# Cross attention 0 of a four-layer decoder: the negated maxima are added on four 32-row tiles, for both halves at once and ahead of the scores

## The chip, the cores and the metric

One NeuronCore of one Trainium2 chip runs the whole program. The metric is the time on the device of one execution, in microseconds (us). The engines of the core work side by side and wait for each other by semaphores: TensorE (PE in the profile, PEld for its weight loads), VectorE (DVE), ScalarE (ACT), GpSimd (POOL) and SyncE (SP), which only issues transfers here.

## The reference, cut to what matters

A decoder of four layers, each with self attention, cross attention and a feed-forward part. The change lies in the cross attention of layer 0: 1024 queries against 6404 keys, 16 heads of 64 numbers.

```python
def _L0_xattn_ref(q_in, k_in, v_in, key_mask, Wq, bq, Wk, bk, Wv, bv, Wo, bo):
    HEADS, QSIZE, KSIZE = (16, 64, 64)
    ...
    qw = (q_in @ Wq + bq).reshape(B, M, HEADS, QSIZE)
    kw = (k_in @ Wk + bk).reshape(B, N, HEADS, QSIZE)
    vw = (v_in @ Wv + bv).reshape(B, N, HEADS, KSIZE)
    a = jnp.einsum('bmhd,bnhd->bhmn', qw, kw) / jnp.sqrt(jnp.float32(QSIZE))
    a = jnp.where(key_mask[:, None, None, :], a, -jnp.inf)
    a = jax.nn.softmax(a, axis=-1)
    o = jnp.einsum('bhmn,bnhd->bmhd', a, vw).reshape(B, M, HEADS * KSIZE)
    return o @ Wo + bo
```

Before each exponential the row's maximum is subtracted. In the kernel the scores stand transposed (keys on partitions, queries along the free axis), so the maximum of a query can't be the bias of an activation. It is added to the scores on TensorE instead.

## The kernel before

The function is `cross_0`. The 16 heads are worked as `P = 8` pairs; the two heads of a pair, `a = 0` and `1`, lie on partitions 0 to 63 and 64 to 127 (`head(a)`). The keys come in `C = 13` chunks of up to 512 (four tiles of 128 keys, the last chunk of a pair has three; 51 tiles for a pair, 408 in all, numbered `t`). The queries come in two halves of 512 (`HALVES`).

The order of the work is written out by hand. `turns()` goes over turns `g`. In turn `g` the chunk `g` of a first pass is done, which finds the maxima from bfloat16 copies of the keys and queries (`maxima`, L2235, eight groups of 128 queries for each chunk, reduced by VectorE in L2417), and beside it chunk `j = g - 14` of the second pass. So turns 0 to 13 hold maxima alone, turns 14 to 103 both, and turns 104 to 117 the second pass alone. A turn has one step `s` for each tile of chunk `j`, usually with two of the eight groups of maxima. For each tile TensorE does:

- `scores(j, s, half)` for both halves: two float32 products of 64 rows (L2248), which run at the same time since they lie on different rows of the array, into banks `2 * half` and `2 * half + 1` of PSUM; then two bfloat16 products of 64 rows (L2250) that add the negated maxima: the stationary operand is `ones`, the moving one `Qa`, which holds the negated maximum of each query as a sum of two bfloat16 numbers in rows 0 and 1 of each head and zeros in the other rows.
- `products(t - 1)` (L2267): the exponentials of the tile before times the values, four float32 products with 64 columns of the array, two at a time.

ScalarE takes the exponential of each half (L2354) into `Pr`, which has four buffers. GpSimd adds it to the running sums `Ps0` (L2474) and `Ps1` (L2483). A group of maxima in turns 14 on uses banks 4 and 5 alone, so that the next one, or the new keys and values (L2274, L2279, in step 0 of each turn), must wait for its reduction. At the end of a turn VectorE merges its maxima (L2449); at the end of a pair's 13 turns it negates them (L2453) and splits them into `mz` (L2457, L2459), and TensorE turns them into rows (L2293), from which `Qa` is copied.

In step 0, and in a step with other work of the pair (queries, rows, sums, output), the second group of maxima stands between the two halves of the scores; in the others it stands behind them. "The usual step" below is one of turns 14 to 103 with no such work.

Of the kernel before, what the change touches and what calls it, by code (L numbers as in the profile page):

```python
# [12 lines left out]
ALU = mybir.AluOpType  # L13
# [12 lines left out]
HALVES = [slice(h * HALF, (h + 1) * HALF) for h in range(S // HALF)]  # L26
# [2137 lines left out]
def cross_0(k, io, X, stack):  # L2164
# [6 lines left out]
    nc, ps, ctx = k.nc, k.ps, k.context  # L2171
# [13 lines left out]
    Kr, Kb = k.tile(stack, "Kr", [128, 16, CHUNK]), k.tile(stack, "Kb", [128, 2, CHUNK], BF16)  # L2185
    Vc = k.tile(stack, "Vc", [128, 3, CHUNK])
    Q, Qb = k.tile(stack, "Q", [128, 3, S]), k.tile(stack, "Qb", [128, 2, S], BF16)
    Qa, ones = k.tile(stack, "Qa", [128, 2, S], BF16), k.tile(stack, "ones", [128, 128], BF16)
# [3 lines left out]
    mx, red, neg = k.tile(stack, "mx", [128, 8, 2]), k.tile(stack, "red", [128, 2, 8, 2]), k.tile(stack, "neg", [128, 8, 2])  # L2192
    mz = k.tile(stack, "mz", [128, 8, 2, 64], BF16)
    ones_f, zero_row = k.tile(stack, "ones_f", [128, 64]), k.tile(stack, "zero_row", [1, HALF], BF16)
    out_bias = k.tile(stack, "out_bias", [128, 1])
    head = lambda a: slice(64 * a, 64 * a + 64)
# [4 lines left out]
    def turns():  # L2201

        for g in range(-1, N + LAG + 3):
            j = g - LAG
            yield g, j, (ctx.tiles_in(j % C) if 0 <= j < N else TPC)

    def maxima_at(g, s, steps):
        return range(8 * s // steps, 8 * (s + 1) // steps) if 0 <= g < N else range(0)

    def maxima_bank(i, q):  # L2210
        return (4, 0, 2)[(8 * i + q) % 3] if i < LAG else 4

    def pair_for(g, s, turn, step):

        p = (g - turn) // C
        return p if s == step and (g - turn) % C == 0 and 0 <= p < P else None

    def pe():
        taken = {0: [], 2: [], 4: []}

        def take_banks(b, *when_free):

            for mark in taken[b]:
                nc.tensor.wait_ge(*mark)
            taken[b] = when_free
# [12 lines left out]
        def scores(j, s, half):  # L2238
            t, p = KT * (j // C) + TPC * (j % C) + s, j // C
            if s == 0 and half == 0:  # L2240
                nc.tensor.wait_ge(*key_set.at(j + 1))
                if j % C == 0:
                    nc.tensor.wait_ge(*query_set.at(p + 1))
                    nc.tensor.wait_ge(*rows_set.at(p + 1))
            take_banks(2 * half, exp_done.at(2 * t + half + 1))
            sl = HALVES[half]
            for a in range(2):
                nc.tensor.matmul(ps[:, 2 * half + a, :], lhsT=Kr[head(a), j % 16, s * 128:(s + 1) * 128], rhs=Q[head(a), p % 3, sl], start=True, stop=False)  # L2248
            for a in range(2):
                mm = nc.tensor.matmul(ps[:, 2 * half + a, :], lhsT=ones[head(a), :], rhs=Qa[head(a), p % 2, sl], start=False, stop=True)  # L2250
            mm.then_inc(*scored.up())

        def products(t):
# [59 lines left out]
        for t in range(P):  # L2313
            mm = nc.tensor.matmul(ps[:, 0, 0:1], lhsT=wo[:, t, :], rhs=bv[:, t:t + 1], start=t == 0, stop=t == P - 1)
# [4 lines left out]
        for g, j, steps in turns():  # L2319
            for s in range(steps):  # L2320
                t = KT * (j // C) + TPC * (j % C) + s
                items = maxima_at(g, s, steps)
                others = [(item, pair_for(g, s, turn, step)) for item, turn, step in
                          ((queries, -1, 1), (rows, C, 1), (sums, LAG + C, 1), (output, LAG + C + 2, 2)) if pair_for(g, s, turn, step) is not None]
                between = 2 if s == 0 or others else 1
                for q in items[:1]:
                    maxima(g, q)
                if 0 <= j < N:
                    scores(j, s, 0)
                for q in items[1:between]:  # L2330
                    maxima(g, q)
                if 0 <= j < N:
                    scores(j, s, 1)
                for q in items[max(1, between):]:
                    maxima(g, q)
                if s == 0:
                    keys_and_values(g + 1, j + 1)
                for item, p in others:
                    item(p)
                if 0 <= j and 0 < t <= KT * P and (j < N or s == 0):  # L2340
                    products(t - 1)
# [55 lines left out]
    def dve():  # L2397
        nc.vector.memset(ones[:], 1.0)
        nc.vector.memset(ones_f[:], 1.0)
        nc.vector.memset(zero_row[:], 0.0).then_inc(*zeroed.up())  # L2400
        nc.vector.memset(mz[:], 0.0).then_inc(*zeroed.up())
        nc.vector.wait_ge(*constant_mm.at(1))
        nc.vector.tensor_tensor(out_bias[:], ps[:, 0, 0:1], bo[:], ALU.add).then_inc(*constant_set.up())
        both = ps[:, 4:6, :]

        def inverse(p, n):
            sl = slice(n * 128, (n + 1) * 128)
            nc.vector.wait_ge(*sums_set.at(p + 1))
            nc.vector.reciprocal(over[:, sl], over[:, sl]).then_inc(*inverse_step.up())

        for g, j, steps in turns():
            for s in range(steps):
                for q in maxima_at(g, s, steps):
                    nc.vector.wait_ge(*maxima_mm.at(8 * g + q + 1))
                    if g >= 2 and q == 0:
                        nc.vector.wait_ge(*merged.at(g - 1))
                    nc.vector.tensor_reduce(red[:, g % 2, q, :], ps[:, maxima_bank(g, q):maxima_bank(g, q) + 2, 0:ctx.keys_in(g % C)], AX, ALU.max).then_inc(*reduced.up())  # L2417
                p = pair_for(g, s, -1, 1)
                if p is not None:
                    nc.vector.wait_ge(*query_mm.at(p + 1))  # L2420
                    if p >= 3:
                        nc.vector.wait_ge(*scored.at(2 * KT * (p - 2)))
                        nc.vector.wait_ge(*query_copied.at(p - 2))
                    nc.vector.tensor_scalar(Q[:, p % 3, :], both.rearrange("p a n -> p (a n)"), bq[:, p:p + 1], scale, ALU.add, ALU.mult).then_inc(*query_set.up())
                for n in range(8):
                    p = pair_for(g, s, LAG + C + (n + 2) // 4, (n + 2) % 4)
                    if p is not None:
                        inverse(p, n)
                p = pair_for(g, s, LAG + C + 2, 1)
                if p is not None:  # L2430
                    nc.vector.wait_ge(*inverse_step.at(9 * p + 8))
                    nc.vector.wait_ge(*acc_copied.at(p + 1))
                    nc.vector.tensor_tensor(Ur[:], Ur[:], over[:], ALU.mult).then_inc(*inverse_step.up())
                p = pair_for(g, s, LAG + C + 2, 2)
                if p is not None:
                    nc.vector.wait_ge(*out_mm.at(p + 1))
                    if p:
                        nc.vector.wait_ge(*x_added.at(p))
                        nc.vector.tensor_tensor(X[:], X[:], both.rearrange("p a n -> p (a n)"), ALU.add).then_inc(*x_added.up())
                    else:  # L2440
                        nc.vector.wait_ge(*constant_set.at(1))
                        nc.vector.scalar_tensor_tensor(X[:], both.rearrange("p a n -> p (a n)"), out_bias[:, 0:1], X[:], ALU.add, ALU.add).then_inc(*x_added.up())
            if 0 <= g < N:
                nc.vector.wait_ge(*reduced.at(8 * (g + 1)))
                if g % C == 0:
                    nc.vector.tensor_copy(mx[:], red[:, g % 2]).then_inc(*merged.up())
                else:
                    nc.vector.wait_ge(*merged.at(g))
                    nc.vector.tensor_tensor(mx[:], mx[:], red[:, g % 2], ALU.max).then_inc(*merged.up())  # L2449
                if g % C == C - 1:  # L2450
                    p = g // C
                    nc.vector.wait_ge(*merged.at(g + 1))
                    nc.vector.tensor_scalar(neg[:], mx[:], -1.0, None, ALU.mult).then_inc(*rows_step.up())  # L2453
                    nc.vector.wait_ge(*rows_step.at(3 * p + 1))
                    if p:
                        nc.vector.wait_ge(*rows_mm.at(p))
                    nc.vector.tensor_copy(mz[:, :, :, 0], neg[:]).then_inc(*rows_step.up())  # L2457
                    nc.vector.wait_ge(*rows_step.at(3 * p + 2))
                    nc.vector.tensor_tensor(mz[:, :, :, 1], neg[:], mz[:, :, :, 0], ALU.subtract).then_inc(*rows_step.up())  # L2459

    def pool():
        for g, j, steps in turns():
# [811 lines left out]
```

## Time and the profile before

| | |
|---|---|
| median of 3 runs | 6965.2 us (6961.23 to 6971.22) |
| the profiled execution, its own time | 6964.83 us |
| its span, first to last instruction | 6963.1 us |
| mean granted TensorE clock | 0.904 of full |
| TensorE busy in the span | 5944.1 us, 85% |
| the second pass of cross attention 0 | from about 697 to 2945 us |

A row of the timeline gives the start (us from the span's start), the time from there to the end of the last instruction merged into it, the engine, line and operation, and the count. Matmuls overlap: one of 512 columns lasts about 0.38 us in the records, but the next starts about 0.21 us after it. So what a matmul costs is read from start to start, not from its own duration. A float32 matmul has two records.

### The profile page before, as it was taken

The numbers are of one execution on the slowest core, as the hardware profiler recorded it, in microseconds if no ns is written. First come the engines' busy times: TensorE is split into PE (matmuls) and PEld (weight loads), VectorE is DVE, ScalarE is ACT, GpSimd is POOL, SyncE is SP. The second block draws the span as 40 slices with busy tenths as digits, with TensorE's granted clock in tenths as the row PEclk, the third lists the DMA queues.
The fourth block names the chain that finished last, engine by engine and source line by source line (L and its number), as shares of the span: only waits on it lengthen the run. The fifth ranks groups of instructions, "written<-read, shape, count | busy, mean of one in ns | idle before, by whom it ended". The sixth has DMA issues, their size and how long they took to land. (4 is left out here: it accounts for less than half of the span.)

```text
span 6963.1 us, 76588 instructions
## 1 busy us (share of the span) xinstructions
PE 5944.1 (85%) x30204; PEld 2276.6 (33%) x30219; DVE 3275.8 (47%) x4563; ACT 3212.5 (46%) x3531; POOL 1903.2 (27%) x845
## 2 busy tenths in 40 slices
PE   8975999999999999979869569998888368888879
PEld 5741333333333333336624121111356111111114
DVE  4557555555555553034363430000232799899813
ACT  3321444444444445422202249998111137777752
POOL 0000878788787889900000000000000000000000
PEclk8875999999999999989989789999776679999979
DMA  1000000000000000000021030000000300000000
GB/s 47 4 13 0 1 1 1 1 1 1 1 1 1 1 1 1 1 28 7 9 92 34 17 101 16 16 9 7 16 30 8 118 1 9 18 9 9 2 17 31
DMA packets 91699, 118.19 MB, mean 17 GB/s; under 512 B 23358, under 2 KB 66729, under 8 KB 89741
## 3 DMA queue, kind: packets, MB, share of 16 engines
q1 hardware_dynamic: 91340, 113.29, 5.2%
q8 instruction: 240, 3.93, 0.2%
q14 instruction: 119, 0.97, 0.0%
HBM read 75.86 MB, written 37.39 MB: 16 GB/s over the span
## 5 line engine op out<-in xcount | busy, mean ns | idle before, releaser
L2417 DVE TENSOR_REDUCE red<-ps 128x2 f32<-128x1024 f32 (+1 forms) x832 | 976.9, 1182 | 965.7 <-PE ps L2235 963.8
L2354 ACT ACTIVATE Pr<-ps,key_bias 128x1024 f32<-128x1024 f32 x816 | 897.5, 1115 | 1112.9 <-PE ps L2250 1112.5
L2474 POOL TENSOR_TENSOR Ps<-Ps,Pr 128x1024 f32<-128x1024 f32 x400 | 944.1, 2360 | 318.0 <-ACT Pr L2354 318.0
L2910 DVE TENSOR_REDUCE red<-ps 128x2 f32<-128x1024 f32 (+2 forms) x1102 | 961.4, 926 | 79.3 <-PE ps L2825 66.2
L2483 POOL TENSOR_TENSOR Ps<-Ps,Pr 128x1024 f32<-128x1024 f32 x400 | 948.4, 2371 | 32.7 <-ACT Pr L2354 32.7
L492 POOL MEMSET sel<- 16x2048 f32 (+1 forms) x2 | 2.7, 1368 | 3402.9 <-POOLq L89 3402.9
L2888 ACT ACTIVATE Pr<-ps 128x1024 f32<-128x1024 f32 x816 | 786.2, 1021 | 224.6 <-PE ps L2835 223.6
L2248 PE MATMUL ps<-Q,Kr 64*128 64x512 f32 x3264 | 851.8, 600 | 0.0
L2267 PE MATMUL ps<-Pr,Vc 128*64 128x512 f32 x3264 | 789.8, 605 | 0.0
L3011 ACT ACTIVATE Pr<-ps 128x1536 f32<-128x1536 f32 x544 | 732.7, 1495 | 2.7 <-PE ps L2977 2.3
L2825 PE MATMUL ps<-Kp,Q 52*128 52x512 bf16 (+1 forms) x1664 | 449.8, 410 | 226.8 <-DVE red L2910 149.3
L2235 PE MATMUL ps<-Kb,Qb 64*128 64x512 bf16 (+1 forms) x1664 | 335.7, 406 | 149.3 <-DVE red L2417 115.4
L2848 PE MATMUL ps<-Pr,V 128*9 128x512 f32 x3264 | 435.0, 605 | 0.0
L2990 PE MATMUL ps<-Pr,V 128*8 128x512 f32 x3264 | 427.1, 596 | 0.2 <-ACT Pr L3011 0.2
L2977 PE MATMUL ps<-Q,Kp 48*128 48x512 bf16 x1632 | 329.3, 385 | 56.9 <-ACT Pr L3011 33.3
L2835 PE MATMUL ps<-Q,Kp 52*128 52x512 bf16 x1632 | 363.5, 386 | 12.2 <-ACT Pr L2888 11.6
L2825 PEld LDWEIGHTS ps<-Kp,Q 52*128 52x128 bf16 x1664 | 107.1, 94 | 799.8 <-DVE red L2910 713.2
L2248 PEld LDWEIGHTS ps<-Q,Kr 64*128 64x128 f32 x3264 | 311.8, 191 | 161.5 <-issue 122.7
L3020 DVE COPY Oc<-ps 128x512 f32<-128x512 f32 x8 | 5.5, 692 | 732.7 <-PE ps L2990 732.7
L2267 PEld LDWEIGHTS ps<-Pr,Vc 128*64 128x64 f32 x3264 | 198.0, 136 | 382.0 <-issue 290.8
L2250 PE MATMUL ps<-Qa,ones 64*128 64x512 bf16 x1632 | 313.3, 380 | 0.0
L2235 PEld LDWEIGHTS ps<-Kb,Qb 64*128 64x128 bf16 x1664 | 80.5, 95 | 665.2 <-DVE red L2417 421.0
(487 smaller groups left out, 6596.9 us busy)
## 6 DMA issues: line engine op xcount, KB each, us to landing
L_dram_K<-parts SPq DMA_DIRECT2D x26, 384.0 KB, 2.8
Kp<-L_dram_K SPq DMA_DIRECT2D x16, 624.0 KB
L_dram_K<-parts SPq DMA_DIRECT2D x26, 256.0 KB, 2.3
Kp<-L_dram_K SPq DMA_DIRECT2D x16, 416.0 KB
w<-L_ffn_experts_w_dram SPq DMA_DIRECT2D x24, 256.0 KB, 3.0
L_dram_V<-Vt SPq DMA_DIRECT2D x13, 258.0 KB, 2.8
Vc<-L_dram_V SPq DMA_DIRECT2D x13, 258.0 KB, 2.7
ctx<-ctx_dram SPq DMA_DIRECT2D x13, 256.0 KB, 5.8
```

The lines of the kernel that those rows point to most:

```text
L2248: nc.tensor.matmul(ps[:, 2 * half + a, :], lhsT=Kr[head(a), j % 16, s * 128:(s + 1) * 128], rhs=Q[head(a), p % 3, sl], start=True, stop=False)
L2267: mm = nc.tensor.matmul(ps[head(a), 6 + half, :], lhsT=Vc[:, j % 3, at:at + 64], rhs=Pr[:, t % 4, half, a, :], start=False, stop=True, ski ...
L2354: nc.scalar.activation(Pr[:, t % 4, half].rearrange("p a n -> p (a n)"), ps[:, 2 * half:2 * half + 2, :].rearrange("p a n -> p (a n)"), AC ...
L2417: nc.vector.tensor_reduce(red[:, g % 2, q, :], ps[:, maxima_bank(g, q):maxima_bank(g, q) + 2, 0:ctx.keys_in(g % C)], AX, ALU.max).then_inc ...
L2474: nc.gpsimd.tensor_tensor(into, into, src, ALU.add).then_inc(*summed0.up())
L2483: nc.gpsimd.tensor_tensor(into, into, src, ALU.add).then_inc(*summed1.up())
L2825: mm = nc.tensor.matmul(ps[:, b + item - first, 0:keys], lhsT=Q[head(a), p, q * 128:(q + 1) * 128], rhs=Kp[head(a), p % 3, at:at + keys], ...
L2848: mm = nc.tensor.matmul(ps[at:at + 9, 6, :], lhsT=A.V[:, kt, 2 * p + a, :], rhs=Pr[:, t % 4, half, a, :], start=False, stop=True, skip_gro ...
L2888: nc.scalar.activation(Pr[:, t % 4, half].rearrange("p a n -> p (a n)"), ps[:, 2 * half:2 * half + 2, :].rearrange("p a n -> p (a n)"), AC ...
L2910: nc.vector.tensor_reduce(red_flat[:, g % 2, first:first + n], ps[:, b:b + n, 0:ctx.keys_in(g % C)], AX, ALU.max).then_inc(*reduced.up())
L2990: mm = nc.tensor.matmul(ps[at:at + 8, 6 + p % 2, :], lhsT=A.V[:, kt, 2 * p + a, :], rhs=Pr[:, i % 18, :], start=False, stop=True, skip_gro ...
L3011: nc.scalar.activation(Pr[:, slot:slot + n, :].rearrange("p a n -> p (a n)"), ps[:, 3 * (u % 2):3 * (u % 2) + n, :].rearrange("p a n -> p ...
```

## The change

All four additions of the negated maxima of a tile (two heads, two halves) are done ahead of the scores, each on a 32-row tile of the array: rows 0 to 31 and 64 to 95 for the first half, 32 to 63 and 96 to 127 for the second. For that the two rows of `mz` are written twice, at 0 and 1 and at 32 and 33. The additions now begin the sum in each bank and the scores end it. The banks of both halves are waited for ahead of the additions.

```diff
-            take_banks(2 * half, exp_done.at(2 * t + half + 1))
-            sl = HALVES[half]
+            if half == 0:
+                take_banks(0, exp_done.at(2 * t + 1))
+                take_banks(2, exp_done.at(2 * t + 2))
+                for quarter in range(4):
+                    x, a = quarter // 2, quarter % 2
+                    rows = slice(64 * a + 32 * x, 64 * a + 32 * x + 32)
+                    nc.tensor.matmul(ps[:, quarter, :], lhsT=ones[rows, :], rhs=Qa[rows, p % 2, HALVES[x]], start=True, stop=False)
             for a in range(2):
-                nc.tensor.matmul(ps[:, 2 * half + a, :], lhsT=Kr[head(a), j % 16, s * 128:(s + 1) * 128], rhs=Q[head(a), p % 3, sl], start=True, stop=False)
-            for a in range(2):
-                mm = nc.tensor.matmul(ps[:, 2 * half + a, :], lhsT=ones[head(a), :], rhs=Qa[head(a), p % 2, sl], start=False, stop=True)
+                mm = nc.tensor.matmul(ps[:, 2 * half + a, :], lhsT=Kr[head(a), j % 16, s * 128:(s + 1) * 128], rhs=Q[head(a), p % 3, HALVES[half]], start=False, stop=True)
             mm.then_inc(*scored.up())
...
-                    nc.vector.tensor_copy(mz[:, :, :, 0], neg[:]).then_inc(*rows_step.up())
+                    twice = neg[:].unsqueeze(3).to_broadcast([128, 8, 2, 2])
+                    parts = mz[:].rearrange("p q a (x r) -> p r q a x", r=32)
+                    nc.vector.tensor_copy(parts[:, 0], twice).then_inc(*rows_step.up())
                     nc.vector.wait_ge(*rows_step.at(3 * p + 2))
-                    nc.vector.tensor_tensor(mz[:, :, :, 1], neg[:], mz[:, :, :, 0], ALU.subtract).then_inc(*rows_step.up())
+                    nc.vector.tensor_tensor(parts[:, 1], twice, parts[:, 0], ALU.subtract).then_inc(*rows_step.up())
```

On TensorE, the order of a step 0 and of the usual step behind it, before the change (L2235 are maxima, L2248 scores, L2250 the additions, L2274 and L2279 new keys and values, L2267 the products):

```order
574 L2235 MATMUL ps<-Kb,Qb 128x512 x2
575 L2248 MATMUL ps<-Q,Kr 128x512 x2
576 L2250 MATMUL ps<-Qa,ones 128x512 x2
577 L2235 MATMUL ps<-Kb,Qb 128x512 x2
578 L2248 MATMUL ps<-Q,Kr 128x512 x2
579 L2250 MATMUL ps<-Qa,ones 128x512 x2
580 L2274 MATMUL ps<-ctx_masked,Wk 128x512
581 L2279 MATMUL ps<-Wv,ctx 128x128 x4
582 L2267 MATMUL ps<-Pr,Vc 64x512 x4
583 L2235 MATMUL ps<-Kb,Qb 128x512 x2
584 L2248 MATMUL ps<-Q,Kr 128x512 x2
585 L2250 MATMUL ps<-Qa,ones 128x512 x2
```

The same two steps on TensorE after the change (L2251 are the additions, L2253 the scores, L2277 and L2282 keys and values, L2270 the products):

```order
553 L2235 MATMUL ps<-Kb,Qb 128x512 x2
554 L2251 MATMUL ps<-Qa,ones 128x512 x4
555 L2253 MATMUL ps<-Q,Kr 128x512 x2
556 L2235 MATMUL ps<-Kb,Qb 128x512 x2
557 L2253 MATMUL ps<-Q,Kr 128x512 x2
558 L2277 MATMUL ps<-ctx_masked,Wk 128x512
559 L2282 MATMUL ps<-Wv,ctx 128x128 x4
560 L2270 MATMUL ps<-Pr,Vc 64x512 x4
561 L2235 MATMUL ps<-Kb,Qb 128x512 x2
562 L2251 MATMUL ps<-Qa,ones 128x512 x4
563 L2253 MATMUL ps<-Q,Kr 128x512 x4
```

The two pairs of additions have become one group of four, between the first maxima and the first scores. In the usual step both halves of the scores now follow each other (L2253 x4), and the group of four stands where the scores of the first half began.

## Rows read from the trace of the kernel before

**Rows 1.** The page: busy time of each engine, and the group of the additions.

```profile
PE 5944.1 (85%) x30204; PEld 2276.6 (33%) x30219; DVE 3275.8 (47%) x4563; ACT 3212.5 (46%) x3531; POOL 1903.2 (27%) x845
...
L2250 PE MATMUL ps<-Qa,ones 64*128 64x512 bf16 x1632 | 313.3, 380 | 0.0
```

**Rows 2.** Stretch and its length, busy PE, PEld, DVE, ACT, POOL, granted clock, DMA.

```profile
965.00:2700.00 1735.00, 1617.35 (x8320) 589.41 (x8318) 905.31 (x781) 823.75 (x860) 1411.02 (x616) 0.99 0.00 1
2750.00:2900.00 150.00, 150.00 (x734) 54.47 (x732) 1.22 (x1) 76.61 (x75) 150.00 (x66) 1.00 0.00 1
```

**Rows 3.** Timeline of a usual step and the start of the next.

```profile
1703.65 0.39 PE L2235 MATMUL ps<-Kb,Qb 64*128 64x512 bf16 x2
...
1703.88 1.02 PE L2248 MATMUL ps<-Q,Kr 64*128 64x512 f32 x4
...
1704.73 0.38 PE L2250 MATMUL ps<-Qa,ones 64*128 64x512 bf16 x2
...
1704.95 1.02 PE L2248 MATMUL ps<-Q,Kr 64*128 64x512 f32 x4
1705.16 2.19 ACT L2354 ACTIVATE Pr<-ps,key_bias 128x1024 f32<-128x1024 f32 x2 [2.42 <-PE ps L2250]
...
1705.81 0.38 PE L2250 MATMUL ps<-Qa,ones 64*128 64x512 bf16 x2
...
1706.03 0.38 PE L2235 MATMUL ps<-Kb,Qb 64*128 64x512 bf16 x2
...
1706.33 1.94 PE L2267 MATMUL ps<-Pr,Vc 128*64 128x512 f32 x8
...
1708.20 0.39 PE L2235 MATMUL ps<-Kb,Qb 64*128 64x512 bf16 x2
```

**Rows 4.** Timeline, TensorE: the step with the one-row products that clear a pair's sums.

```profile
706.21 0.40 PE L2235 MATMUL ps<-Kb,Qb 64*128 64x512 bf16 x2
706.54 0.60 PE L2260 MATMUL ps<-zero_row 1*128 1x512 bf16 x2
707.07 1.94 PE L2267 MATMUL ps<-Pr,Vc 128*64 128x512 f32 x8
```

**Rows 5.** Timeline, TensorE: a step of the second pass alone.

```profile
2933.44 1.13 PE L2248 MATMUL ps<-Q,Kr 64*128 64x512 f32 x4
2934.40 0.38 PE L2250 MATMUL ps<-Qa,ones 64*128 64x512 bf16 x2
...
2937.66 0.70 PE L2248 MATMUL ps<-Q,Kr 64*128 64x512 f32 x2
```

**Rows 6.** Timeline of a step 0, with VectorE and GpSimd around it.

```profile
1694.54 2.36 POOL L2474 TENSOR_TENSOR Ps<-Ps,Pr 128x1024 f32<-128x1024 f32 x1
...
1695.77 1.16 DVE L2449 TENSOR_TENSOR mx<-mx,red 128x16 f32<-128x16 f32 x1
...
1696.27 0.39 PE L2235 MATMUL ps<-Kb,Qb 64*128 64x512 bf16 x2
...
1696.85 1.21 DVE L2417 TENSOR_REDUCE red<-ps 128x2 f32<-128x1024 f32 x1
...
1698.12 0.39 PE L2235 MATMUL ps<-Kb,Qb 64*128 64x512 bf16 x2 [0.39 <-DVE red L2417]
...
1699.83 1.12 PE L2274 MATMUL ps<-ctx_masked,Wk 128*128 128x512 f32 x2 [0.25 <-DVE red L2417]
...
1706.35 2.36 POOL L2474 TENSOR_TENSOR Ps<-Ps,Pr 128x1024 f32<-128x1024 f32 x1 [2.52 <-ACT Pr L2354]
...
1708.66 2.35 POOL L2483 TENSOR_TENSOR Ps<-Ps,Pr 128x1024 f32<-128x1024 f32 x1
```

**Rows 7.** Timeline: the last sums of the second pass.

```profile
2951.81 3.68 PE L2302 MATMUL ps<-Ps,ones_f 128*64 128x512 f32 x8 [8.15 <-POOL Ps L2483]
```

**Rows 8.** Timeline: the end of a pair's maxima.

```profile
952.86 2.29 DVE L2457 CAST mz<-neg 128x16 bf16<-128x16 f32 x1
...
956.57 0.61 PE L2235 MATMUL ps<-Kb,Qb 64*128 64x512 bf16 x2 [5.50 <-DVE red L2417]
```

## The prediction

> **What bounds the kernel now.** I read the page first, then busy time by stretch, then the timeline of single steps. The page gives the size of what is changed: 1632 additions of the negated maxima, in pairs, so 816 starts on TensorE [rows 1]. In 965 to 2700 us, where both passes run, TensorE is busy 1617 of 1735 us, GpSimd 1411, VectorE 905 and ScalarE 824; in 2750 to 2900 us, where the second pass runs alone, both TensorE and GpSimd are busy all 150 us [rows 2]. These are two limits, and the change is worth something else in each.
>
> In the usual step TensorE waits for nobody. From start to start [rows 3]: first maxima to scores 0.23 us, scores of a half 0.85 or 0.86 (four passes, two at a time, 0.43 each), additions 0.22, scores 0.86, additions 0.22, and 2.38 from the first maxima to the second. Then 0.30 to the products and 1.87 for them; 4.55 in all. The exponentials of the tile end at 1707.35 (1705.16 + 2.19) and the next step starts at 1708.20, so ScalarE has 0.85 us in hand there.
>
> In step 0 it is another engine. The second maxima stand 1.85 us behind the first (1696.27, 1698.12) and new keys 1.71 behind those (1699.83), both with an idle time that a reduction ended, since only one pair of banks is left for maxima [rows 6].
>
> **What a change of tile shape costs.** Additions cost 0.22 from start to start where they stand among scores of the same shape [rows 3]. Maxima (64 rows by 128 columns) to products (128 by 64) takes 0.30, not 0.22. The nearest row to what the change brings is another: maxima to a one-row product, whose tile is 32 rows high, 706.21 to 706.54, 0.33 us (the second of the two maxima is 0.02 late there, so 0.31), and from the second of the one-row pair (which run one after the other, 0.60 for the two less 0.38 for one, so it starts 0.22 later) at 706.76 to the products 0.31 [rows 4]. So going over to a 32-row tile costs about 0.09 more than an ordinary step, as does leaving it. A float32 product that comes first after such a change also shows its weight load: in the second pass alone the first half's scores take 0.96 (2933.44 to 2934.40) against 0.85 [rows 3, 5]; 0.10 more. The first bfloat16 pair behind a change takes 0.01 more (0.23 against 0.22) [rows 3].
>
> The row shows a change from 64 to 32 rows that costs as much as one to column tiles. The Trainium skill, "TensorEngine Tiling (Array Packing)", Key Properties, says that changing the tiling mode, not just the tile, drains TensorE: by that rule the change pays two drains for each tile, and the trace agrees with 0.09 us for one. The page "TensorE: Matmul & The Clock Gate" of the Trainium skill, Measured speedup vs the span model, gives 3.07 times for four row tiles of 32 rows, not 4; an estimate by it would be 4 x 0.22 / 3.07 = 0.28 us for the group of four, 0.06 more than I take, 14 us over 240 steps.
>
> **The change part by part.**
>
> *The additions.* Removed: one start of 0.22 in each tile, since four run at once and not two by two. The trace has no four row tiles at once. Lower bound of the group: 0.22, as for a pair whose two members start within 0.01 of each other; upper bound: two pairs one after the other 0.44, or four singles 0.86, as the one-row pair runs when both use the same rows [rows 4]. These four use four different quarters of the rows and four banks, so I take 0.22 and keep 0.44 for the range.
>
> *The changes of shape.* Added: 0.09 into the 32-row tiles and 0.09 out, 0.10 for the weight load of the float32 scores that is now bare, 0.01 for the first bfloat16 group: 0.29. By the second decimals above, first maxima to second maxima goes from 2.38 to 0.32 + 0.32 + 0.96 + 0.86 = 2.46 or 2.47. Net **+0.09 us for a usual step**; the removal is worth less than the two changes of shape it brings.
>
> *How many such steps.* Turns 14 to 103 are 90 chunks, six pairs of 51 tiles and 12 chunks of four, 354 tiles. 90 are step 0; 24 have other work (queries, rows, sums, output, six each). That leaves 240, and the trace has 240 steps of the pattern of rows 3. 240 x 0.09 = **+22 us**.
>
> *Step 0 and steps with other work.* The path on TensorE from first to second maxima goes from 1.30 to 0.32 + 0.32 + 0.96 = 1.60 or 1.61. It is still below 1.85, so the reduction hides it; if the group of four took 0.44 it would be 1.83, just hidden too. From second maxima to new keys TensorE has 0.22 less work, which lengthens the wait for the reduction and gives nothing. **0 us.** The steps of the chunks with 260 keys have short reductions: about +0.1 in each of some seven, below 1 us.
>
> *GpSimd behind it.* Once per chunk GpSimd runs dry and starts again with the first exponential of step 1 (idle 2.52 before 1706.35); from there each sum takes 2.31 (1706.35 to 1708.66) [rows 6]. The merge of the maxima at the end of the turn lasts 1.16 us, until GpSimd's running sum ends at 1696.90 (1694.54 + 2.36), and the reduction of step 0 starts with that end, at 1696.85, 0.58 behind its maxima. From the second maxima to the new keys, with nothing else in the way of the reduction, it is 1.71 in all; from the first to the second it is 1.85, so the merge makes it 0.14 late. This is the path that sets step 0. After the change the first scores are ready 0.31 later behind the first maxima (1.61 against 1.30), so GpSimd starts 0.31 later in each chunk; and a step of 4.64 is now longer than two sums, 4.62, so it waits 0.02 to 0.04 more in each of two steps. Its sum then ends 0.31 to 0.38 later in a chunk, where the three TensorE steps alone give 0.09 x 2.67 = 0.24. I add 0.07 in 90 chunks: **+6 us**, between 0 and 12.
>
> *The second pass alone.* 54 tiles. There the step leaves one shape and enters another anyway and the bare load is there already: -0.22 + 0.09 + 0.01 + small = -0.11 for TensorE, 54 x 0.11 = -6 us. But its last sums waited 8.15 us for GpSimd [rows 7], which is busy throughout [rows 2] at 4.62 a tile against TensorE's 4.22 (2933.44 to 2937.66) [rows 5]. TensorE will wait 14 us and not 8. **0 us**; if GpSimd were not there, -6.
>
> *The wait for both halves.* The additions wait for both exponentials of the tile before; behind them on TensorE stand all scores of the tile, and ScalarE waits for those. In the usual step they are done 0.85 + 0.32 = 1.17 us ahead of the additions, and in the second pass alone 0.64 ahead (they start 0.43 behind the additions [rows 3], so 2934.40 + 0.43 + 2.19 = 2937.02 against 2937.66 [rows 5]). No time; were the cover gone, it would be up to one exponential, 1.1, in each tile.
>
> *VectorE.* `mz` is written with 32 numbers and not 16, eight times. The cast took 2.29 us at the end of a pair for 16 numbers, since it waits until a sum of GpSimd ends, and TensorE then waited 5.50 for the reduction behind it [rows 8]. Some 16 more numbers are hundredths of a us. If the repeated source took the cast out of that wait, it would give back up to 2.1 x 6 = 13 us; I see no reason that it should. **0 us**, between -13 and 0.
>
> *The sum*: 22 + 0 + 6 + 0 = +28 us. The profiled execution took 6964.83 us, 0.4 below the median of 6965.2, so 6964.8 + 28 = **6993 us**, 0.4% slower. Less than 0.2% (14 us) can't be told from no change here.
>
> **The rivals.**
>
> - *The four don't run at once* (two and two, or each start later). For it: nothing in the trace shows four. Against: pairs on separate rows start within 0.01. At 0.44 the usual step has +0.31: 240 x 0.31 = 74, plus 6, 7045 us; one after another beyond 7150. Chance 0.10 for the first and 0.02 for the second; another 0.1 for a part of it, 0.03 to 0.08 a group, 7000 to 7015.
> - *Faster: rows can be re-tiled without a stop* (only column tiles would cost it). Then both 0.09 and the bare load fall away and the usual step has 0.22 less: 240 x -0.22 = -53, 6912 us. It decides from the point where two changes and the load cost less than 0.22. Against it stand the 0.31 into and out of the one-row product [rows 4]. Chance 0.04; 0.02 more for the mix of it with a cheaper cast.
> - *No change: the load is not bare* (the float32 weights go in beside the additions, which use other quarters at their turn), or one of the two stops is hidden. Then the usual step has -0.01 to 0.00, and what is left is GpSimd's later start and noise: 6964 to 6975 us. For it: the way out of 32-row tiles into float32 scores is nowhere in the trace. Against: each first float32 product behind a change shows it [rows 5]. Chance 0.11.
> - *The change as forecast*: 0.61.
>
> **How the numbers follow.** The time is that of the likeliest case, whose own range is 6984 to 7002. The range of 8 in 10 leaves out the faster case, most of the "no change" case (together below 6974: 0.10) and the two-and-two case above 7025 (0.10): 6974 to 7025. Slower by over 0.2% (above 6979): forecast and the rival of the four, 0.83; same 0.11; faster 0.06.
>
> **What the profile will show.** In the usual step: four additions that start within about 0.02 of each other; maxima to additions and additions to scores 0.32 each; the first pass of the scores 0.53 and the second 0.43; a step of 4.64. In step 0 the same 1.85 to 1.9 and 1.71. The last sums wait some 14 us for GpSimd. The cast of `mz` near 2.3. The prediction is wrong if the additions start one after the other, or if they stand 0.22 from their neighbours.

## The result, and the profile after

| | before | after |
|---|---|---|
| median | 6965.2 us (6958.39 to 6971.49, 7 runs) | 6992.56 us (6986.86 to 7017.58, 7 runs) |
| profiled execution: span | 6963.1 us | 6990.9 us |
| first maxima of cross attention 0 start | 530.5 us | 521.6 us |
| second pass: first scores to last sums | 696.7 to 2954.4, 2257.7 us | 688.3 to 2983.6, 2295.3 us |

The ratio is 1.0048, 95% interval 1.0033 to 1.0064: slower by 23 to 45 us. (It is taken over all runs; the two medians alone stand at 1.0039.) The prediction was 6993, the median is 6992.6. But the two profiled spans differ by 27.8 us while their second passes differ by 37.6; the difference is luck outside it: the first maxima started 8.9 us earlier in the execution after, behind instructions that the change doesn't touch. So by the traces the change itself costs about 38 us, within the interval, and the sum of 28 was 10 short.

The timeline of a usual step and a step 0 after the change (start, length, engine, line, operation; L2251 are the additions, L2253 the scores, L2270 the products, L2452 the merge, L2479 and L2488 GpSimd's sums):

```profile
1696.50 2.36 POOL L2479 TENSOR_TENSOR Ps<-Ps,Pr 128x1024 f32<-128x1024 f32 x1 [2.81 <-ACT Pr L2357]
...
1702.78 0.39 PE L2235 MATMUL ps<-Kb,Qb 64*128 64x512 bf16 x2
1703.11 0.39 PE L2251 MATMUL ps<-Qa,ones 32*128 32x512 bf16 x4
...
1703.43 1.99 PE L2253 MATMUL ps<-Q,Kr 64*128 64x512 f32 x8
...
1705.25 0.38 PE L2235 MATMUL ps<-Kb,Qb 64*128 64x512 bf16 x2
1705.56 1.94 PE L2270 MATMUL ps<-Pr,Vc 128*64 128x512 f32 x8
...
1705.80 2.36 POOL L2479 TENSOR_TENSOR Ps<-Ps,Pr 128x1024 f32<-128x1024 f32 x1
1706.93 1.26 DVE L2452 TENSOR_TENSOR mx<-mx,red 128x16 f32<-128x16 f32 x1
1707.43 0.39 PE L2235 MATMUL ps<-Kb,Qb 64*128 64x512 bf16 x2
1707.76 0.39 PE L2251 MATMUL ps<-Qa,ones 32*128 32x512 bf16 x4
1708.08 1.13 PE L2253 MATMUL ps<-Q,Kr 64*128 64x512 f32 x4
...
1708.12 1.21 DVE L2420 TENSOR_REDUCE red<-ps 128x2 f32<-128x1024 f32 x1
...
1709.38 0.39 PE L2235 MATMUL ps<-Kb,Qb 64*128 64x512 bf16 x2 [0.17 <-DVE red L2420]
...
1711.09 1.13 PE L2277 MATMUL ps<-ctx_masked,Wk 128*128 128x512 f32 x2 [0.46 <-DVE red L2420]
```

Against [rows 3]: the four additions end 0.39 us after the first of them starts, and one alone lasts 0.385 by the median, so they start together; in the trace's records the fourth starts 0.010 us behind the first. But their neighbours stand 0.33 and 0.32 away, not 0.22. From first to second maxima it is 2.47 (1702.78 to 1705.25) and was 2.38; the step is 4.65 and was 4.55. Against [rows 6]: the second maxima of step 0 stand 1.95 behind the first and stood 1.85; the new keys 1.71 behind those, as before. GpSimd's sum that the merge waits for ends at 1708.16 (1705.80 + 2.36), 0.73 behind the first maxima; it was 0.63.

The end of the second pass, in the timeline of the changed kernel:

```profile
2980.96 3.55 PE L2305 MATMUL ps<-Ps,ones_f 128*64 128x512 f32 x8 [13.44 <-POOL Ps L2488]
```

TensorE waits 13.44 us for GpSimd where it waited 8.15 [rows 7]: it got through the stretch with the second pass alone faster, and that went into the wait.

### The profile page after: what moved, and what is told of

Same layout as the page of the kernel before. It is cut to its first block and busy times, and to the rows that moved or that the text cites. A ratio compares the mean times of both kernels' runs of the same rounds, so it can differ in the third digit from the quotient of the medians.

```text
span 6990.9 us, 76892 instructions
## 1 busy us (share of the span) xinstructions
PE 5961.3 (85%) x30204; PEld 2234.0 (32%) x30219; DVE 3287.6 (47%) x4563; ACT 3189.9 (46%) x3531; POOL 1909.1 (27%) x845
## 5 line engine op out<-in xcount | busy, mean ns | idle before, releaser
L2357 ACT ACTIVATE Pr<-ps,key_bias 128x1024 f32<-128x1024 f32 x816 | 876.0, 1112 | 1147.3 <-PE ps L2253 1146.1
L2479 POOL TENSOR_TENSOR Ps<-Ps,Pr 128x1024 f32<-128x1024 f32 x400 | 945.7, 2364 | 353.9 <-ACT Pr L2357 353.9
L2488 POOL TENSOR_TENSOR Ps<-Ps,Pr 128x1024 f32<-128x1024 f32 x400 | 949.7, 2374 | 30.5 <-ACT Pr L2357 30.5
L2253 PE MATMUL ps<-Q,Kr 64*128 64x512 f32 x3264 | 840.8, 623 | 0.0
L2270 PE MATMUL ps<-Pr,Vc 128*64 128x512 f32 x3264 | 789.8, 605 | 0.0
L2235 PE MATMUL ps<-Kb,Qb 64*128 64x512 bf16 (+1 forms) x1664 | 335.1, 405 | 134.4 <-DVE red L2420 100.5
L2253 PEld LDWEIGHTS ps<-Q,Kr 64*128 64x128 f32 x3264 | 284.0, 189 | 242.5 <-issue 239.3
L2270 PEld LDWEIGHTS ps<-Pr,Vc 128*64 128x64 f32 x3264 | 198.0, 136 | 436.3 <-issue 342.1
L843 PE MATMUL ps<-Q,K 128*128 128x512 f32 (+3 forms) x576 | 283.9, 594 | 7.0 <-DVE K L872 7.0
L813 PEld LDWEIGHTS ps<-V,A 128*128 128x128 f32 x1728 | 259.8, 216 | 82.1 <-issue 68.8
```

Of the source, the lines that this page charges most:

```text
L2253: mm = nc.tensor.matmul(ps[:, 2 * half + a, :], lhsT=Kr[head(a), j % 16, s * 128:(s + 1) * 128], rhs=Q[head(a), p % 3, HALVES[half]], star ...
L2270: mm = nc.tensor.matmul(ps[head(a), 6 + half, :], lhsT=Vc[:, j % 3, at:at + 64], rhs=Pr[:, t % 4, half, a, :], start=False, stop=True, ski ...
L2357: nc.scalar.activation(Pr[:, t % 4, half].rearrange("p a n -> p (a n)"), ps[:, 2 * half:2 * half + 2, :].rearrange("p a n -> p (a n)"), AC ...
L2479: nc.gpsimd.tensor_tensor(into, into, src, ALU.add).then_inc(*summed0.up())
L2488: nc.gpsimd.tensor_tensor(into, into, src, ALU.add).then_inc(*summed1.up())
```

## The experiments

For the experiments the second pass is measured inside one trace, from the first start of the scores to the last start of the sums (rows of L2302 and its like, read to 0.1 us), since nothing outside it can blur that. There is one trace for each kernel, so a difference of a us or two in this column says nothing by itself. "Product to product" is the time from the start of one tile's products to those of the next, by kind of step, the median over all such steps of a trace: in the usual step 4.554 before and 4.650 after the change (239 steps), in step 0 7.384 and 7.475 (83 steps). The six steps 0 of about 14 us, behind the end of a pair's maxima, are left out of the 83.

| kernel | median | ratio to before, 95% | second pass | against before | usual step | step 0 |
|---|---|---|---|---|---|---|
| before | | | 2257.7 | | 4.55 | 7.38 |
| the change | 6992.56 | 1.0048 (1.0033 to 1.0064) | 2295.3 | +37.6 | 4.65 | 7.48 |
| e1, order alone | 6974.21 | 1.0021 (1.0007 to 1.0034) | 2278.0 | +20.3 | 4.55 | 7.61 |
| e2, ahead of the maxima | 6967.7 | 1.0017 (1.0002 to 1.0031) | 2271.9 | +14.2 | 4.45 | 7.81 |
| e3, two groups | 7125.09 | 1.0245 (1.0223 to 1.0266) | 2432.7 | +175.0 | 5.16 | 7.24 |
| e4, always ahead | 6963.27 | 1.0019 (1.0000 to 1.0038) | 2268.4 | +10.7 | 4.45 | 7.81 |
| n1, before, one merge | 6941.82 | 0.9983 (0.9971 to 0.9995) | 2247.7 | -10.0 | 4.55 | 7.24 |
| n2, change, one merge | 6974.43 | 1.0022 (1.0009 to 1.0036) | 2270.8 | +13.1 | 4.65 | 7.24 |
| n3, e2 with one merge | 6927.77 | 0.9956 (0.9940 to 0.9973) | 2222.5 | -35.2 | 4.45 | 7.24 |
| n4, e4 with one merge | 6941.94 | 0.9981 (0.9964 to 0.9998) | 2247.5 | -10.2 | 4.45 | 7.57 |

The kernel before had a median of 6959.96 us beside e1 to e4 and 6954.44 beside n1 to n4; the ratios are to those.

### e1: the order without the small tiles

```diff
-                    rows = slice(64 * a + 32 * x, 64 * a + 32 * x + 32)
-                    nc.tensor.matmul(ps[:, quarter, :], lhsT=ones[rows, :], rhs=Qa[rows, p % 2, HALVES[x]], start=True, stop=False)
+                    nc.tensor.matmul(ps[:, quarter, :], lhsT=ones[head(a), :], rhs=Qa[head(a), p % 2, HALVES[x]], start=True, stop=False)
```

and `mz` written as before the change.

> All four additions stand ahead of the scores and wait for both halves, as in the change, but on 64-row tiles (two pairs, mz written once), so no change of shape is added. Theory A (shape changes and GpSimd's later start): first to second maxima stays 2.38 us and the usual step 4.55, the first scores are ready 1.52 instead of 1.30 behind the first maxima, so GpSimd starts 0.22 later in each chunk and carries it into the merge and step 0: 90 x 0.22 = +20 us on before, about 6985. Theory B (shape changes alone, GpSimd plays no part): +0 to +3, about 6966. Theory C (it is the place ahead of the scores and the wait for both halves that costs, not the shape): as the changed kernel, 6993 or more, with an idle time before the additions that an exponential ended.

The timeline of e1, a usual step and a step 0 (L2250 the additions, L2252 the scores, L2269 the products, L2451 the merge):

```profile
1700.22 0.39 PE L2235 MATMUL ps<-Kb,Qb 64*128 64x512 bf16 x2
1700.44 0.59 PE L2250 MATMUL ps<-Qa,ones 64*128 64x512 bf16 x4
...
1702.59 0.38 PE L2235 MATMUL ps<-Kb,Qb 64*128 64x512 bf16 x2
...
1703.27 2.35 POOL L2476 TENSOR_TENSOR Ps<-Ps,Pr 128x1024 f32<-128x1024 f32 x1
1704.27 1.37 DVE L2451 TENSOR_TENSOR mx<-mx,red 128x16 f32<-128x16 f32 x1
1704.77 0.39 PE L2235 MATMUL ps<-Kb,Qb 64*128 64x512 bf16 x2
...
1705.57 1.21 DVE L2419 TENSOR_REDUCE red<-ps 128x2 f32<-128x1024 f32 x1
...
1706.84 0.39 PE L2235 MATMUL ps<-Kb,Qb 64*128 64x512 bf16 x2 [0.39 <-DVE red L2419]
```

TensorE's usual step is what it was, 4.55 (1700.22 to 1704.77). Yet step 0 grew by 0.22, to 7.61: its second maxima now stand 2.07 behind the first. The reduction starts at 1705.57, when the merge is through; the merge is 1.37 long and was 1.16 [rows 6], because GpSimd's sum ends 0.85 behind the first maxima and not 0.63. The second pass grew by 20.3 us where theory A said 20 and B said 0 to 3; by the ratio it is 5 to 24 us. C, the wait for both halves, falls: the usual step, which has the wait, did not grow, and the changed kernel cost 17 us more than this one with the same waits. So the order alone costs 20 us, and by way of GpSimd. It isn't a part of the 38 that could be taken off: in the changed kernel the usual steps are longer, GpSimd catches up in them, and step 0 grew by 0.09 and not by 0.22.

That the merge is long because of GpSimd is shown within the trace before, too. These are all merges (L2449) and the same instruction of the next cross attention (L2916), where GpSimd has no work; count, then shortest, median and longest in ns:

```profile
L2449 DVE TENSOR_TENSOR mx<-mx,red x96: 174/1160/2220, 554.4 to 2693.8; 128x16 f32<-128x16 f32 x96
L2916 DVE TENSOR_TENSOR mx<-mx,red x96: 174/175/177, 5551.1 to 6594.5; 128x16 f32<-128x16 f32 x96
```

Of the 96 merges, 84 began while GpSimd was on a sum, and every one of them ended within 0.06 us of the end of that sum; the 12 others, in the first turns, lasted 0.17 or 0.18 us.

### e2: the small tiles where the shape changes anyway

```diff
+                ahead = between == 1
+                if 0 <= j < N and ahead:
+                    additions(j, s)
                 for q in items[:1]:
                     maxima(g, q)
                 if 0 <= j < N:
+                    if not ahead:
+                        additions(j, s)
                     scores(j, s, 0)
```

where `additions` holds the four additions and their waits.

> As the change, but in the usual step the four additions stand ahead of the first maxima, right behind the products, where the tile shape changes anyway and bfloat16 maxima, not float32 scores, come behind them; in the steps with maxima between the halves they stay where the change puts them. Shape rule: products to additions 0.53, additions to maxima 0.32, maxima to scores 0.22, no bare float32 load: the usual step is 4.44, 0.11 below before. Theory A (a chunk's length is set by GpSimd from its start in step 1 to the merge): the first scores of step 1 are ready 0.10 later behind the products than before, so the chunk is 0.0 to 0.1 longer in spite of the shorter steps: 6965 to 6975. Theory B (the steps on TensorE add up): 240 x -0.11 = -26, about 6939.

The timeline of e2 (L2247 the additions, L2256 the scores, L2273 the products, L2460 the merge):

```profile
1706.63 1.94 PE L2273 MATMUL ps<-Pr,Vc 128*64 128x512 f32 x8
...
1708.50 0.39 PE L2247 MATMUL ps<-Qa,ones 32*128 32x512 bf16 x4
1708.82 0.39 PE L2235 MATMUL ps<-Kb,Qb 64*128 64x512 bf16 x2
1709.05 1.88 PE L2256 MATMUL ps<-Q,Kr 64*128 64x512 f32 x8
...
1711.66 2.35 POOL L2487 TENSOR_TENSOR Ps<-Ps,Pr 128x1024 f32<-128x1024 f32 x1
1712.45 1.59 DVE L2460 TENSOR_TENSOR mx<-mx,red 128x16 f32<-128x16 f32 x1
1712.95 0.39 PE L2235 MATMUL ps<-Kb,Qb 64*128 64x512 bf16 x2
...
1715.23 0.39 PE L2235 MATMUL ps<-Kb,Qb 64*128 64x512 bf16 x2 [0.51 <-DVE red L2428]
```

Additions to maxima 0.32, maxima to scores 0.23 as before the change, usual step 4.45: 0.20 below the changed kernel for one change of shape (0.09) and one bare float32 load (0.10) less. But the steps 0 took it back: 7.81 instead of 7.38, with 2.28 from first to second maxima. Three steps shorter by 0.105 and one longer by 0.43 make a chunk 0.11 longer than before. The second pass is 14.2 us above before where theory B had -26 and A 0 to +10. A's mechanism holds; its size was a little low, since the turns in which a pair's sums are made grew too (6.3 us in six steps, not foreseen).

### e3: the suspected cost doubled

```diff
-            if half == 0:
-                take_banks(0, exp_done.at(2 * t + 1))
-                take_banks(2, exp_done.at(2 * t + 2))
-                for quarter in range(4):
...
+            take_banks(2 * half, exp_done.at(2 * t + half + 1))
+            for a in range(2):
+                rows = slice(64 * a + 32 * half, 64 * a + 32 * half + 32)
+                nc.tensor.matmul(ps[:, 2 * half + a, :], lhsT=ones[rows, :], rhs=Qa[rows, p % 2, HALVES[half]], start=True, stop=False)
```

> The suspected cost doubled: each half's two additions on 32-row tiles right ahead of its own scores, so four changes of shape in a tile for two and two bare float32 loads for one, and the additions take 0.22 twice as before the change. Theory of the shape changes: first to second maxima 2.38 + 2 x 0.29 = 2.96 us, the usual step 5.13, 240 x 0.58 = +139, with GpSimd's later start 7105 to 7130. If the cost in the changed kernel is one per tile whatever the number of changes (a wait, or four tiles at once): +20 to +60, below 7030.

The timeline of e3, one usual step (L2248 the additions, L2250 the scores, L2267 the products):

```profile
1707.46 0.39 PE L2235 MATMUL ps<-Kb,Qb 64*128 64x512 bf16 x2
1707.78 0.39 PE L2248 MATMUL ps<-Qa,ones 32*128 32x512 bf16 x2
...
1708.10 1.13 PE L2250 MATMUL ps<-Q,Kr 64*128 64x512 f32 x4
1709.16 0.39 PE L2248 MATMUL ps<-Qa,ones 32*128 32x512 bf16 x2
1709.48 1.13 PE L2250 MATMUL ps<-Q,Kr 64*128 64x512 f32 x4
1710.44 0.38 PE L2235 MATMUL ps<-Kb,Qb 64*128 64x512 bf16 x2
```

2.98 from maxima to maxima (2.96 expected), a usual step of 5.16 (5.13). The cost is one per change of shape. The scores of both halves now take 0.96 or 1.06 to what follows: 1709.48 to 1710.44 with the bare load alone, 1708.10 to 1709.16 with the load and the next change of shape. Two additions at once cost the same 0.32 to 1709.48 as four did, so four at once cost no more than two. And step 0 fell to 7.24, below before: a usual step of 5.16 is longer than its two sums on GpSimd, 4.62, so GpSimd's backlog at the merge is gone. The same 7.24 comes back in n1 to n3.

The time, 7125 us, lies in the range (7105 to 7130), but in part by luck. The second pass grew by 175 us where the expectation has 140 to 165. The usual steps brought 146 and the stretch with the second pass alone some 13, its last wait counted in; steps 0 gave 23 back, which was not foreseen, and the six steps with an output grew by 26, from 8.27 to 12.6 each, which was not foreseen either. There VectorE's product for the output waits for GpSimd's second sum (L2433 lasts 3.23 us and not 1.23). In the step from 1694 us on it ends at 1697.98, 1.08 behind the end of that sum; TensorE then stands idle for 3.01 us, and over 1699 to 1705.5 us, behind that, its granted clock is 0.53 where it was 1.00 ahead of it: the lower of its two levels (1.2 and 2.4 GHz) for most of the stretch. The steps of e3 show the price of a change of shape; its total does not.

### e4: ahead of the maxima in step 0 too

```diff
-                ahead = between == 1
+                ahead = True
```

> As e2, but the additions stand ahead of the first maxima in every step, in step 0 too, where they lengthen the path from the products to the first maxima by 0.32 us. Theory A (GpSimd's running sum holds up the merge and so the reduction of step 0): later first maxima in step 0 meet a merge that is late anyway, the two paths are nearly equal, and it is within 5 us of e2. Theory B (TensorE's steps add up): 90 x 0.32 = 29 us above e2.

The second pass is 2268.4 against e2's 2271.9, step 0 7.81 in both: 0.32 us more ahead of the first maxima in each of 90 steps changed nothing while the merge is what step 0 waits for. Theory A allowed 5 us either way, theory B had 29. The medians, 6963.27 and 6967.7, agree.

### n1 to n4: the merge made once for a pair

If the merge ties step 0 to GpSimd, taking it out must separate all these kernels by what TensorE does. In each, the reductions of a pair's 13 turns go to places of their own, and one reduction at the end takes their maximum:

```diff
-                if g % C == 0:
-                    nc.vector.tensor_copy(mx[:], red[:, g % 2]).then_inc(*merged.up())
-                else:
-                    nc.vector.wait_ge(*merged.at(g))
-                    nc.vector.tensor_tensor(mx[:], mx[:], red[:, g % 2], ALU.max).then_inc(*merged.up())
                 if g % C == C - 1:
                     p = g // C
-                    nc.vector.wait_ge(*merged.at(g + 1))
+                    nc.vector.wait_ge(*reduced.at(8 * (g + 1)))
+                    nc.vector.tensor_reduce(mx[:], red[:, p % 2].rearrange("p c q a -> p q a c"), AX, ALU.max).then_inc(*merged.up())
+                    nc.vector.wait_ge(*merged.at(p + 1))
```

> The kernel before, but each turn's reduced maxima go to a place of their own and are merged once for each pair of heads, by one reduction, instead of once for each turn by an elementwise maximum that waits for GpSimd. Same result. Theory A (the merge ties step 0 to GpSimd's running sum): step 0 goes from 7.38 to 7.24 us, the usual step stays 4.55, and it is 12 to 25 us faster than before, 6940 to 6950. Theory B (the merge costs nothing on the path): no change.

Step 0 is 7.24, as expected to the hundredth, the usual step 4.55. The second pass gained 10.0 us, below A's 12 to 25, and the ratio 0.9983 is 12 us (3 to 20): A's direction and mechanism, with a gain at or under its low end.

> The changed kernel with the one merge for each pair. Theory A: usual step 4.65, step 0 7.24 as in the kernel before without merges; what is left of the change is 240 x 0.096 = 23 us and a few more in the steps with other work, so 20 to 32 above the kernel before without merges, near 6970; the +8 us in the 83 steps 0 are gone. Theory B (step 0 grew for another reason, such as the shape changes in it): step 0 stays 0.09 longer than in the kernel before without merges.

Step 0 of n2, with GpSimd, in its timeline (L2475 and L2484 the sums, L2277 the new keys):

```profile
1699.07 2.36 POOL L2475 TENSOR_TENSOR Ps<-Ps,Pr 128x1024 f32<-128x1024 f32 x1
1700.70 0.39 PE L2235 MATMUL ps<-Kb,Qb 64*128 64x512 bf16 x2
...
1701.13 1.23 DVE L2420 TENSOR_REDUCE red<-ps 128x2 f32<-128x1024 f32 x1 [0.97 <-PE ps L2235]
1701.35 1.13 PE L2253 MATMUL ps<-Q,Kr 64*128 64x512 f32 x4
...
1702.42 0.39 PE L2235 MATMUL ps<-Kb,Qb 64*128 64x512 bf16 x2
...
1704.13 1.12 PE L2277 MATMUL ps<-ctx_masked,Wk 128*128 128x512 f32 x2 [0.46 <-DVE red L2420]
```

The reduction starts 0.43 behind its maxima, in the middle of a sum of GpSimd (1699.07 to 1701.43); it reads PSUM and waits for nobody. First to second maxima 1.72. Step 0 is 7.24 in n2 as in n1, so all 8 us that the change cost there came through the merge; B falls. What is left of the change is 2270.8 - 2247.7 = 23.1 us (20 to 32 expected), as much as the usual steps alone grew (23.0).

> The additions ahead of the first maxima in the usual step, as before, with one merge for each pair. Theory A: now nothing ties step 0 to GpSimd, so the gain of the usual steps (4.45 against 4.55) is kept and step 0 is 7.24: 25 us below the kernel before without merges, 35 to 50 below before, 6910 to 6930. Theory B (the exponentials or something else lengthen step 0 when the others get shorter): step 0 stays near 7.8 and the time near before.

The second pass is 2222.5, 25.2 below n1 (25 expected), with a usual step of 4.45 and a step 0 of 7.24: now the gain of the four tiles is kept. The ratio is 0.9956 (0.9940 to 0.9973), 31 us faster than the kernel before, somewhat less than the 35 to 50 expected, though the second pass has 35.2. Of all kernels here this one is the fastest.

> As the one before, with the additions ahead of the first maxima in step 0 too. Theory A: with the merge gone the first maxima of step 0 are on the path, so the additions' 0.32 us there shows: step 0 7.56, some 90 x 0.32 = 25 to 30 us above the kernel before this one, although with merges the two kernels were within 5 us. If they stay equal, it wasn't the merge that hid it.

The same edit that was worth nothing between e2 and e4 costs 25.0 us between n3 and n4 (2222.5 to 2247.5; 25 to 30 expected), step 0 7.57 against 7.24. The merge had hidden it.

## Why the prediction was right

**The additions, four at once, 0.22.** Right. 0.385 us each and 0.39 for all four; with pairs in e3 the same 0.32 to the next. The two-and-two rival is out. The Trainium skill's 3.07 times ("TensorE: Matmul & The Clock Gate", Measured speedup vs the span model) would have made it 0.29 by an estimate, 4 x 0.22 / 3.07 (the prediction wrote 0.28); here the measurement decides for 0.22, since first to second maxima is 2.47 and would be some 2.53 by the other.

**Two changes of shape and one bare load, 0.29 for 0.22 saved.** Right: +0.096 in each usual step, 22.9 us over them where the sum had 22. e3 has the cost twice, e2 one change of shape more than the kernel before and no bare load, e1 neither. The rule of the Trainium skill ("TensorEngine Tiling (Array Packing)", Key Properties) that a change of mode drains the array agrees: 0.09 us for it, from 64 rows to 32 as from rows to columns. The rival of no change, a hidden load, is out too.

**Step 0 and GpSimd, +6.** The mechanism was right and is shown by e1, e4, n1, n2 and n4; the size was 8.4 us in 83 steps, 0.09 to 0.10 a chunk where the prediction had 0.07, between 0 and 0.14. The sign that it named for step 0, second maxima 1.85 to 1.9 behind the first, was missed by a little: they stand 1.95 behind.

**Steps with other work, 0.** This is the term that was mis-sized: +6.6 us. Product to product, the six steps with the sums of a pair grew by 3.7 us in all, those with the output by 1.3, and those with the queries by 0.6 (0.1 each, as a usual step); the rows step by nothing. The six steps 0 of about 14 us grew by 1.0 in all, but single ones by -0.7 to +0.7, which is scatter. With one merge for each pair (n2 against n1) the sums' part is gone, 1.33 against 1.30 us over before, so that was the merge again. The output's 1.3 stays in n2. The traces show where it comes from; here is the first of these steps, before and then after the change (L2433 and L2436 are VectorE's product for the output):

```profile
1035.44 2.35 POOL L2474 TENSOR_TENSOR Ps<-Ps,Pr 128x1024 f32<-128x1024 f32 x1 [2.53 <-ACT Pr L2354]
...
1037.30 0.39 PE L2235 MATMUL ps<-Kb,Qb 64*128 64x512 bf16 x2
...
1037.66 1.23 DVE L2433 TENSOR_TENSOR Ur<-Ur,over 128x1024 f32<-128x1024 f32 x1
...
1038.80 1.22 DVE L2417 TENSOR_REDUCE red<-ps 128x2 f32<-128x1024 f32 x1
```

```profile
1034.48 2.36 POOL L2479 TENSOR_TENSOR Ps<-Ps,Pr 128x1024 f32<-128x1024 f32 x1 [2.82 <-ACT Pr L2357]
...
1036.12 0.39 PE L2235 MATMUL ps<-Kb,Qb 64*128 64x512 bf16 x2
...
1036.48 1.45 DVE L2436 TENSOR_TENSOR Ur<-Ur,over 128x1024 f32<-128x1024 f32 x1
...
1037.85 1.21 DVE L2420 TENSOR_REDUCE red<-ps 128x2 f32<-128x1024 f32 x1
```

VectorE's product for the output starts 0.36 behind the first maxima in both, but GpSimd's sum ends 0.49 behind them before and 0.72 after. In both the product ends 1.09 or 1.10 behind the end of that sum. So it is 0.22 longer after the change, and the reduction behind it, for which the second maxima wait, starts 0.23 later, in all six steps alike. So this too is GpSimd's later start. No run takes this product away, so the cause is read from the traces and not tried.

**The second pass alone, 0.** Right: TensorE's step fell by 0.104 (4.217 to 4.112), 5.4 us over the 54 tiles, and it waited 13.44 us instead of 8.15.

**VectorE, 0.** Right: the cast of twice as many numbers lasts 2.325 us by the median against 2.293, the subtraction 0.298 against 0.232.

**The wait for both halves, 0.** Right: additions that waited for an exponential did so for 19.5 us in 24 cases, as the scores before did; e1 shows it.

So 22.9 + 8.4 + 6.6 = 37.9 in the second pass, where 28 was forecast. That the median came out at the forecast's number to 1 us is luck: the sum was 10 us short, and the profiled execution after the change, which is the median one, happened to be quicker outside the second pass. By the interval, 23 to 45, both 28 and 38 are possible, and the trace says it is the upper half.

## What to carry to other kernels

Before small matmuls are packed onto smaller tiles, count the changes of tile shape this adds and look at what stands behind each: here one start of 0.22 us was saved and 0.29 paid, and the same four additions made the step 0.10 shorter than before when they stood where the shape changed anyway, ahead of a bfloat16 product. An engine with an idle time once in each turn, as GpSimd here, can still set the turn's length if a small instruction elsewhere waits for it: a gain or a loss on TensorE then shows not at all (e4) or with the other sign (e2). Take that one wait out first, as in n1 to n4, and the rest of the experiments read as sums.

## What the runs showed of the hardware

A VectorE maximum of 16 numbers per partition, both inputs in SBUF, lasts 0.17 us where GpSimd has no work. While GpSimd was on a sum it lasted 1.16 us before [rows 6], 1.26 after the change, 1.37 in e1 and 1.59 in e2, in each to within 0.03 us of the end of that sum. VectorE's product of two inputs in SBUF for the output was held in the same way, 1.45 us after the change and 3.23 in e3 against 1.23 before. A reduction from PSUM was not held up (it started 0.43 behind its maxima in n2 and lasted 1.23, though a sum of GpSimd was on when it started).

A change of tile shape cost much the same, 0.31 to 0.33 us from start to start, instead of 0.22, into 32-row tiles, out of them, and from maxima to products.

Identical work took different times from one execution to the next: the start of the first maxima, behind the same instructions in every kernel, lay between 520.9 us (e4) and 538.7 us (e2), and the time from the last sums to the end between 3987 us (e3) and 4010 us (e2). Over 0 to 400 us the granted clock of e4 was 0.87 and that of e2 0.83, both between its two levels. Ten or twenty us in the time of one execution of a 7 ms program can be this, which is why the second pass was measured inside the trace.
